# Turning a cross-attention stage: keys on partitions, or queries on partitions with the weights transposed by DMA

## The reference, cut to what matters

```python
# x (16, 100, 128), ctx_1024 (16, 1444, 128), 16 heads of 64
xn = layernorm(ctx, ln1_w, ln1_b)              # context, 1444 keys
ln = layernorm(x, ln2_w, ln2_b)                # 100 latents
q = (ln @ Wq).reshape(b, -1, 16, 64)
k, v = split(xn @ Wkv)
q = q * (1 + scale) + shift                    # per batch and head
attn = softmax(einsum('bihd,bjhd->bhij', q, k) * 64 ** -0.5)
out = einsum('bhij,bjhd->bihd', attn, v).reshape(b, -1, 1024) @ Wout
x = layernorm(x + out)
```

## Time and profile before

| | |
|---|---|
| time, median of 3 runs | 1476.45 us (1475.62 to 1478.27) |
| profiled execution | 1476.72 us, its span 1474.9 us |
| PE busy | 1300.3 us (88%) |
| VectorE busy | 1158.3 us (79%) |
| ScalarE busy | 833.5 us (57%) |
| GpSimd busy | 610.6 us (41%) |
| DMA queue of all transfers | 9.9% of 16 engines |
| cross stage, first score matmul to last layer norm | 125.2 to 1163.2 us |
| mean granted TensorE clock | 0.903 |

### The profile page before, as it was taken

How to read it: one execution, slowest core, us unless ns; L and a number is a source line. 1 busy time by engine, 2 the same in 40 slices (tenths; PEclk the granted TensorE clock), 3 DMA queues, 4 the chain that set the end, 5 groups by cost and what they waited for, 6 DMA issues and landing times. The chain is left out here.

```text
span 1474.9 us, 25355 instructions
## 1 busy us (share of the span) xinstructions
PE 1300.3 (88%) x9254; PEld 829.2 (56%) x9254; DVE 1158.3 (79%) x3204; ACT 833.5 (57%) x1346; POOL 610.6 (41%) x419
## 2 busy tenths in 40 slices
PE   3668999999999999999999999999999564877788
PEld 2553555555555555555555555555555453766778
DVE  4967787888888787888878788888875349999994
ACT  0344775757677675867667675766756362222221
POOL 3242646546464654636465563646454110000000
PEclk9667999999999999999999999999999785666666
DMA  7020101201010210101011010101000300000000
GB/s 141 1 43 1 43 20 25 43 1 43 1 43 2 42 40 4 43 1 43 1 43 33 11 43 1 43 1 23 12 12 1 94 0 1 1 6 5 5 5 9
DMA packets 68213, 34.25 MB, mean 23 GB/s; under 512 B 53525, under 2 KB 65657, under 8 KB 67961
## 3 DMA queue, kind: packets, MB, share of 16 engines
q1 hardware_dynamic: 68088, 32.62, 9.9%
HBM read 19.21 MB, written 0.82 MB: 14 GB/s over the span
## 5 line engine op out<-in xcount | busy, mean ns | idle before, releaser
L806 POOL TENSOR_TENSOR p_lo<-e,p_hi 128x800 f16<-128x800 f32 x208 | 385.3, 1859 | 409.8 <-ACT p_hi L887 409.7
L933 DVE TENSOR_REDUCE mxp<-ps 128x1 f32<-128x481 f32 (+1 forms) x624 | 399.1, 654 | 146.8 <-PE ps L1045 132.1
L884 ACT ACTIVATE e<-ps 128x800 f32<-128x800 f32 (+1 forms) x384 | 316.9, 825 | 217.4 <-PE ps L1092 209.6
L887 ACT ACTIVATE p_hi<-ps 128x800 f16<-128x800 f32 (+1 forms) x384 | 318.3, 829 | 0.0
L1090 PE MATMUL ps<-q_hi,xT_hi 128*128 128x400 f16 x704 | 235.4, 334 | 5.6 <-ACT p_hi L887 4.6
L1045 PE MATMUL ps<-xT_hi,q_hi 128*128 128x481 f16 (+1 forms) x624 | 235.0, 377 | 5.0 <-DVE mxp L933 2.7
L1118 PE MATMUL ps<-p_lo,xa_hi 128*128 128x400 f16 x704 | 234.1, 332 | 1.0 <-POOL p_lo L806 1.0
L1092 PE MATMUL ps<-q_hi,xT_lo 128*128 128x400 f16 x704 | 234.7, 333 | 0.0
L1091 PE MATMUL ps<-q_lo,xT_hi 128*128 128x400 f16 x704 | 234.7, 333 | 0.0
L1114 PE MATMUL ps<-p_hi,xa_hi 128*128 128x400 f16 x704 | 234.4, 333 | 0.0
L1115 PE MATMUL ps<-p_hi,xa_lo 128*128 128x400 f16 x704 | 234.1, 332 | 0.0
(11 more groups left out here) (235 smaller groups left out, 2060.2 us busy)
## 6 DMA issues: line engine op xcount, KB each, us to landing
raw<-in_ctx SPq DMA_DIRECT2D x16, 704.0 KB
f_wq<-in_L_ffn_w_q SPq DMA_DIRECT2D x1, 1024.0 KB, 4.9
f_wqt<-in_ffn_wq_t SPq DMA_DIRECT2D x2, 512.0 KB, 7.5
x_tok<-in_x SPq DMA_DIRECT2D x1, 800.0 KB
out_x<-ost SPq DMA_DIRECT2D x6, 128.0 KB, 1.8
raw<-in_ctx SPq DMA_DIRECT2D x32, 18.0 KB
wk_t<-in_wk_t SPq DMA_DIRECT2D x1, 512.0 KB, 5.5
wq_t<-in_wq_t SPq DMA_DIRECT2D x1, 512.0 KB, 7.7
```

The source lines that it names most:

```text
L806: pool.tensor_tensor(out=p_lo[t % P_SLOTS][:, k, :], in0=e32[t % E_SLOTS][:, k, :], in1=p_hi[t % P_SLOTS][:, k, :], op=ALU.subtract).then_ ...
L884: act.activation(e32[t % E_SLOTS][:, half, :], s_banks(t, half), ACT.Exp).then_inc(exp_done, 1)
L887: act.activation(p_hi[t % P_SLOTS][:, half, :], s_banks(t, half), ACT.Exp).then_inc(exp_done, 1)
L933: dve.tensor_reduce(mxp[:, mt, c:c + 1], src[:, 0:MCUT[c + 1] - MCUT[c]], AX_X, ALU.max).then_inc(work_dve, 1)
```

## The change

The cross stage is rewritten with **queries on partitions**. A batch is 13 tiles of 128 queries (the last takes 64 new ones) against all 1444 keys.

- `scores(t)`: `q_hi` or `q_lo` is the weights, the keys are the moving columns: three pieces of 512, 512 and 420, three matmuls each, into three PSUM banks (two such sets).
- The maximum is now one VectorE reduction of the tile (`maximum`) and a second, 1-column instruction that adds `HEADROOM`; ScalarE adds it as `bias` in the exponential. The jobs "M" and "R" are gone, and with them L1045, L933, L1053, L943.
- ScalarE: `exponent` (PSUM to `e32`) and `high_half` (a copy of `e32` to float16 in SBUF). `low_half` is on VectorE for 9 tiles and on GpSimd for 4 (`POOL_LO`).
- `values` contracts over keys, so the weights `p` (128 queries x 2 x 1536 float16) are transposed by one DMA for each tile (`turn_weights`) into a ring of 6 `pT`; then 36 matmuls of 128 columns. There are 2 `e32` and 3 `p` buffers.
- All side jobs use one PSUM bank; a job waits until the one before it was taken. "q" and "Y" stand in fixed slots of the tile order. A tile's value sums share a bank in groups of four tiles, which ScalarE empties.
- `context_norm` moves from VectorE to GpSimd; statistics are taken a batch earlier; the context's last 36 rows are loaded once and not twice.

```diff
-AHEAD = 9
-def side_work(first, last):
...
-LEAD = 4
-E_SLOTS, P_SLOTS = 4, 6
-POOL_TILES = ((0, 2, 5, 8, 10), (0, 2, 3, 4, 5, 6, 8, 10))
...
+LAG = 4
+RING = 6
+E_BUF, P_BUF, N_BUF = 2, 3, 4
+GT = 4
+POOL_LO = (1, 4, 7, 10)
+Q_SLOTS = (1, 6, 9, 10)
+Y_SLOTS = (8, 12, NM, NM + 3, NM + 4, NM + 5)
+Y_HEADS = tuple(tuple(range(h, min(h + 3, H))) for h in range(0, H, 3))
+STAT_SLOTS = (7, 10, 11)
...
+            def turn_weights(t):
+                rows = tile_rows(t % NM)
+                sp.wait_ge(lo_pool if t % NM in POOL_LO else lo_dve, lo_of(t))
+                if t >= RING:
+                    sp.wait_ge(pv_done, t - RING + 1)
+                sp.dma_start_transpose(pT[:, t % RING, :, 0:rows.stop - rows.start],
+                                       p[t % P_BUF][rows, :, :].rearrange("q h k -> q (h k)")).then_inc(pT_ld[t % RING], 16)
...
+            for t in range(ALL_TILES):
+                b, i = divmod(t, NM)
+                turn_weights(t)
+                if i == 5 and b + 3 < B:
+                    sp.wait_ge(xh_done, b + 2)
+                    context_load(sp, cx, a, Batch(None, b + 3))
+                if i == 6 and b + 1 < B:
+                    turn_context(b + 1, 0, xa_hi_done)
+                if i == 7 and b + 1 < B:
+                    turn_context(b + 1, 1, xa_lo_done)
...
         @block.gpsimd
         def _(pool):
...
+            for t in range(ALL_TILES + DRAIN):
+                b, i = divmod(t, NM)
...
+                if t < ALL_TILES and i in POOL_LO:
+                    low_half(t)
+                for kind, of, g in jobs_of(t):
+                    if kind == "q":
+                        queries_lo(of, g)
...
+                if i == 3 and more:
+                    context_rstd(pool, cx, nhalf, Batch(None, b + 1))
+                    for part in range(3):
+                        context_norm(pool, cx, Batch(None, b + 1), part)
+                if i == 5 and more:
+                    context_lo(pool, cx, Batch(None, b + 1))
...
         @block.scalar
         def _(act):
+            def exponent(t):
+                rows = tile_rows(t % NM)
+                act.wait_ge(bias_done, t + 1)
+                if t >= E_BUF:
+                    act.wait_ge(lo_pool if (t - E_BUF) % NM in POOL_LO else lo_dve, lo_of(t - E_BUF))
+                act.activation(e32[t % E_BUF][rows, :], score_banks(t)[rows, 0:T], ACT.Exp,
+                               bias=bias[rows, t % N_BUF:t % N_BUF + 1]).then_inc(e_done, 1)
+
+            def high_half(t):
+                rows = tile_rows(t % NM)
+                if t >= P_BUF:
+                    act.wait_ge(pT_ld[(t - P_BUF) % RING], 16 * ((t - P_BUF) // RING + 1))
+                act.wait_ge(e_done, t + 1)
+                act.activation(p[t % P_BUF][rows, 0, 0:T], e32[t % E_BUF][rows, :], ACT.Copy).then_inc(hi_done, 1)
...
+            for t in range(ALL_TILES + DRAIN):
+                b, i = divmod(t, NM)
+                if t < ALL_TILES:
+                    exponent(t)
+                v = t - LAG
+                if 0 <= v < ALL_TILES and group_end(v):
+                    take_values(v)
+                asked = [j for j in jobs_of(t) if j[0] == "q"]
+                for _, of, g in asked:
+                    take_queries(of, g)
+                if t < ALL_TILES:
+                    high_half(t)
+                for _, of, g in asked:
+                    queries_hi(of, g)
+                if i == 5 and b + 1 < B:
+                    context_hi(act, cx, Batch(None, b + 1))
...
         @block.vector
         def _(dve):
+            def maximum(t):
+                rows, k = tile_rows(t % NM), t % N_BUF
+                dve.wait_ge(s_rdy, t + 1)
...
+                dve.tensor_reduce(nmax[rows, k:k + 1], score_banks(t)[rows, 0:T], AX_X, ALU.max, negate=True).then_inc(max_done, 1)
+                dve.wait_ge(max_done, t + 1)
+                dve.tensor_scalar(bias[rows, k:k + 1], nmax[rows, k:k + 1], HEADROOM, None, ALU.add).then_inc(bias_done, 1)
...
+            for t in range(ALL_TILES + DRAIN):
+                b, i = divmod(t, NM)
+                if t < ALL_TILES:
+                    maximum(t)
+                if 0 < t <= ALL_TILES and (t - 1) % NM not in POOL_LO:
+                    low_half(t - 1)
+                for kind, of, g in jobs_of(t):
+                    if kind == "Y":
+                        take_heads(of, g)
+                if i in STAT_SLOTS and b + 2 < B:
+                    context_stats(dve, cx, Batch(None, b + 2), STAT_SLOTS.index(i))
+                if i == 2 and b + 1 < B:
+                    context_stats(dve, cx, Batch(None, b + 1), 3)
...
         @block.tensor
         def _(pe):
...
+            def scores(t):
...
+                if t >= 2:
+                    pe.wait_ge(e_done, t - 1)
+                q0 = tile_first_query(i)
+                hi, lo = q_hi[b % 2][:, q0:q0 + P], q_lo[b % 2][:, q0:q0 + P]
+                for c in range(0, T, 512):
+                    keys = slice(c, min(c + 512, T))
+                    out = score_banks(t)[:, keys]
+                    pe.matmul(out, hi, xT_hi[b % 2][:, keys], start=True, stop=False)
+                    pe.matmul(out, lo, xT_hi[b % 2][:, keys], start=False, stop=False)
+                    last = pe.matmul(out, hi, xT_lo[b % 2][:, keys], start=False, stop=True)
+                last.then_inc(s_rdy, 1)
+
+            def values(t):
+
+                b, i = divmod(t, NM)
+                pe.wait_ge(pT_ld[t % RING], 16 * (t // RING + 1))
+                if i % GT == 0 and t:
+                    pe.wait_ge(u_done, group_number(t))
...
+                for n in range(NTILE):
+                    hi, lo = xa_hi[b % 2][:, n, :], xa_lo[b % 2][:, n, :]
+                    ph, pl = pT[:, t % RING, n, 0:w], pT[:, t % RING, NTILE + n, 0:w]
+                    pe.matmul(out, hi, ph, start=n == 0, stop=False)
+                    pe.matmul(out, lo, ph, start=False, stop=False)
+                    last = pe.matmul(out, hi, pl, start=False, stop=n == NTILE - 1)
+                last.then_inc(pv_done, 1)
...
+            for t in range(ALL_TILES + DRAIN):
+                if t < ALL_TILES:
+                    scores(t)
+                if 0 <= t - LAG < ALL_TILES:
+                    values(t - LAG)
+                for j in jobs_of(t):
+                    job(*j)
```

More of the change, by code:

```diff
@@ L595, in context_lo @@
     if bt.off >= 2:
-        pool.wait_ge(c.pv_done, bt.val(2 * NTILE, -2 * NTILE))
+        pool.wait_ge(c.pv_done, NM * (bt.off - 1))
     pool.tensor_tensor(out=c.xa_lo[bt.par][:, :, :], in0=c.xh[:, :, :], in1=c.xa_hi[bt.par][:, :, :],
                        op=ALU.subtract).then_inc(c.xa_lo_done, 1)
-AHEAD = 9
-def side_work(first, last):
[L610 to L630, removed]
@@ new lines, in tile_rows, with tile_first_query, lo_of, jobs_of @@
+def tile_rows(i):
+    return slice(0, P) if i < NM - 1 else slice(P - LAST, P)
+def tile_first_query(i):
+    return min(i * P, HQ - P)
+def lo_of(t):
+    b, i = divmod(t, NM)
+    pool = b * len(POOL_LO) + sum(k <= i for k in POOL_LO)
+    return pool if i in POOL_LO else t + 1 - pool
+def jobs_of(t):
+    if t < 0:
+        return [("q", 0, g) for g in range(4)] if t == -1 else []
+    b, i = divmod(t, NM)
+    out = []
+    for g, s in enumerate(Y_SLOTS):
+        if i == s % NM and 0 <= b - s // NM < B:
+            out.append(("Y", b - s // NM, g))
+    for g, s in enumerate(Q_SLOTS):
+        if i == s and b + 1 < B:
+            out.append(("q", b + 1, g))
+    return out
@@ L775, in one_batch, with turn_context @@
[L775 to L782 removed]
+            def turn_context(b, half, made):
+                sp.wait_ge(made, b + 1)
+                if b >= 2:
+                    sp.wait_ge(s_rdy, NM * (b - 1))
+                dst, src = ((xT_hi, xa_hi), (xT_lo, xa_lo))[half]
+                sp.dma_start_transpose(dst[b % 2][:, :].rearrange("d (n q) -> d n q", q=P),
+                                       src[b % 2][:, :, :].rearrange("q n d -> q (n d)")).then_inc(xT_ld, 16)
@@ L1130, in one_batch @@
-            def one_batch(bt, first, last):
-                w, nx = Works(bt, first, last), bt.next()
-                for u in range(2):
-                    for n in range(NTILE):
-                        todo = [k for k, _ in w.at((u, n))]
-                        t3 = NTILE * u + n + LEAD
-                        sb_, st = (bt, t3) if t3 < 2 * NTILE else (nx, t3 - 2 * NTILE)
-                        ahead = not (last and t3 >= 2 * NTILE)
-                        for part in range(4):
-                            if part < 2:
-                                values(bt, u, n, part)
-                            elif ahead:
-                                scores(sb_, st // NTILE, st % NTILE, part - 2)
-                            take_n = -(-len(todo) // (4 - part))
-                            for k in todo[:take_n]:
-                                work(bt, nx, w, k)
```

(1 more changed line is left out.)

581 lines of the change are left out of this document (165 added, 416 removed).

## The result

The change made the kernel slightly slower. Over six runs each, the median went from 1476.95 us (1475.62 to 1478.62) to 1483.05 us (1482.18 to 1484.89); the ratio is 1.0042, with a 95% interval from 1.0029 to 1.0055. The forecast was 1381 us with 0.68 on faster. The time lies inside the range of 1325 to 1520, but 102 us above the forecast, and no rival with a time of its own (1591, 1445, 1333) is near it. The profiled execution took 1482.66 us, its span is 1480.3.

The account below looks back on a forecast made before the run. TensorE was taken to bound the kernel before; after, its 53.9 us plus 5.1 of waits made 59.0 us a batch. With 106 at the start and 17.5 at the end the stage saved 95.7: 1381 us, range 1325 to 1520.

Parts of the forecast that it names:

- 1591: Rival time in us: weight transposes queued behind one another bound the stage, 72 us a batch; chance of slower 0.29.
- 1333: Rival time in us, or less: TensorE alone bounds with hardly a wait, 56 us a batch or less; chance 0.06.
- I take 0.45: Price in us of one `context_norm` instruction on GpSimd, taken between 0.34 and 0.47; 5.4 us a batch.
- Sum 30, and it hides behind everything: GpSimd's work in a batch, 30 us, claimed to cost no time of its own.
- At 1 us each it would no longer hide, and up to 5 us a batch appear: Caveat on GpSimd's norms ahead of `low_half(4)`: at 1 us each, up to 5 us a batch added.
- rival on `bias`: VectorE's one-column `bias`, ahead of every exponential, waits for GpSimd: 63 us a batch, 1445 us; chance 0.15.
- good end: Weight transposes stream at 208 GB/s, 3.8 us a tile; with `raw`, DMA takes 52.9 us a batch.
- hole of the starting pair: 1.3 us gap within the two queued transposes at the kernel's start, taken as no rule for the stage.
- pair's price: Cost of the two queued transposes at the start, 5.2 us for 786 KB (151 GB/s); 72 us a batch.
- 88% busy: TensorE's share at full clock in the new stage, from 114,000 columns in 59 us.
- The clock could fall: TensorE's clock might drop because it waits more often; given no chance of its own.
- Break-even: Batch length at which the change gains nothing: 65.0 us, or 4.67 us a tile for transposes; chance 0.03.

Follow-up runs that it names:

- experiment 6: Changed kernel with four norms moved behind `low_half(4)`, context splitting and transposes a slot later, power in slot 1, `Y`'s last norm in slot 7: 1409.08 us, ratio 0.9531.
- experiment 1: Changed kernel with `context_norm` put back on VectorE in slots 3, 4 and 5, power still on GpSimd: 1483.98 us, ratio 1.0055 to the kernel before.

## Why the prediction was wrong

**The step that failed** is GpSimd's: "I take 0.45", "Sum 30, and it hides behind everything", since "`low_half(4)`, next in its queue, waits for ScalarE until about when the norm ends". A norm takes 0.82 us alone and 0.91 in the batch above (10.96/12), above the upper bound of 0.47. That bound was a two-input instruction of 127 elements by the price of an element; for so short an instruction the rows measure 1.7 times as much alone and nearly twice as much in the batch. The sum over the batch, 34 us of 65, is still harmless; the order is not. The sentence "At 1 us each it would no longer hide, and up to 5 us a batch appear" had the right mechanism and nearly the size: `low_half(4)` was 4.8 us late, and 65.0 - 60.0 = 5.0 us lie between twelve norms and four, the hold of VectorE included. But it was given no chance among the rivals.

**VectorE.** The operations were priced well: maximum 1661 ns for 1665, `bias` 153 for 145, low half 1653 for 1660. What was missing is its holds behind GpSimd: 1.0 us a batch was allowed, and L884 alone averages 2281 over 144 instead of 1653, 5.7 us a batch, with L547 and L915 some 2 more (means 1932 and 882 ns for 174 and 341 alone). The earlier trace rows had shown L580 once at 3632; it was used for the rival on `bias` and not for the low halves, which read two operands from SBUF. The Trainium skill, "SBUF — State Buffer", section "SBUF: two separate sides", lets a VectorE instruction with two SBUF inputs be shut out for the length of a GpSimd instruction. The trace agrees, and shows in addition a hold over three of them in a row, 6.4 us, in 14 batches.

**The rival on `bias`** (1445) is dead: 208 instructions of 150 to 155 ns. But L547, with twelve elements a partition, waits 2 us in most batches; in experiment 6, where GpSimd has nothing running beside it, it takes 173 ns in the mean. The runs do not say where between one element and twelve this begins.

**The transposes.** Neither the good end nor the rival was right. The landing is 6.0 us in the middle, within the 5.5 to 9 given. But the hole of the starting pair did repeat, against "a hole once is no rule": in experiment 6's first line above, four slices from 485.75 us on move 3 to 9 GB/s, one more 52 and the next three 286 to 295, the pattern of the earlier trace rows, and elsewhere the stream is at some 217. What did not repeat is the pair's price: with holes and bursts together the mean is 187, not 151, so 1591 falls. And 208 GB/s, from one 0.3 us stretch with an empty queue, is not what the stage sustains: 174 at 65.0 us a batch, where waits set the pace, and 187 to 188 at 60.4, where 52.9 was reckoned. So, as an estimate, with the norm at its price of 0.45 and every wait as reckoned, the forecast of 59.0 would still have been 1.4 us a batch, 22 us in all, too low. The 261 GB/s of the Trainium skill, "DMA: Bandwidth & Descriptors", section "Latency and other measured facts", is exceeded in bursts (286 to 295 GB/s for 0.75 us in that line) and sustained over 390 us in no run. The 266 GB/s of the window 612 to 615 us are no figure for it: the 0.74 MB load of `raw`, issued at 610.90, runs in them.

**TensorE.** The pitches held (0.056 us for 128 columns), and 57 us busy at a clock of 0.95 (57 x 0.95 = 54) fits the 53.9 of its sum. The "88% busy" of the prediction comes out neither of its 114,000 columns at 0.43 ns (49 us, 83% of 59) nor of its sum (53.9, 91%); nothing else rests on it. "The clock could fall ... I give it nothing of its own" held only as long as no gap grew: after the 6.3 us gap it cost 1.5 us a batch. "Granted clock under 1 in the stage" and "GpSimd's norm over 0.5 us each" were both among its signs of being wrong, and both came.

**ScalarE and the ends.** Exponential 1465 ns for 1380, copy 1407 for 1450. Start 3.2 us late, tail 4.6 us long, and what follows the stage 315.9 us for 313.5: 10.2 us that the forecast missed besides the batches.

**Break-even** was put at a batch of 65.0, and there the kernel ended, by a path that the forecast knew and gave no chance. That the time fell inside the range is luck: its upper side was made for transposes that bind, and they did not bind here.

**Open:** what makes VectorE late with the norm on it (experiment 1) was read from its trace, not tested; how much of the 6.0 us is the hold and how much the lateness is known only in part (2.0 us for 3.6 of the 6.4 us of hold); and why the transposes stream at some 217 GB/s in some slices, at 290 in others and stop for a microsecond between was not tested.

## What to carry to other kernels

When work moves to an engine with idle time, look past its sum, at what stands directly behind the moved block in its queue and who waits for that: here twelve cheap instructions ahead of one that the tile chain needs, and two more behind it, cost 61 us over the kernel; moving the last one behind by a slot gave 29 us back and splitting the twelve around it 32, with nothing removed. Price a short instruction by a row of a short instruction, and give a chance to the case just beyond your bound if its cost is steep. A mean DMA share of 1.00 does not say that the transfers bind, nor even that they never stop (it was 0.01 from 664.3 to 666.0 us); halve the bytes and see, in the version where the other waits are gone as well.

## What the runs showed of the hardware

- A GpSimd `tensor_scalar` of 127 elements a partition with two per-partition operands takes 0.81 to 0.82 us where nothing holds it, on 36 partitions as on 128; VectorE takes 0.33, ScalarE's activation 0.48 in the mean.
- A VectorE instruction with two SBUF operands can be held over several GpSimd instructions that follow without a gap: 8.09 us for 1.65. (The DMA share of 0.01 from 664.3 to 666.0 us is not its doing: the next transpose in the queue is tile 4's, issued at 667.26 when GpSimd's late low half has ended.)
- A one-element `tensor_scalar` (153 ns) is never held, a twelve-element one (174 ns alone) mostly is with GpSimd at work (2155 in the middle).
- DMA transposes of 786 KB, issued one after the other: 187 GB/s over 390 us at a share of 1.08, 6.2 us from issue to landing in the middle. In slices of 0.25 us they run at some 217 GB/s, stop for about 1 us (3 to 9 GB/s) and go on at 286 to 295.
